# Scores of four heads together in the second cross-attention: 32-row groups, four banks for one group, eight probability buffers

## The reference

```python
EMBED, HEADS, HEAD_DIM = 256, 16, 16
q = proj(query, Wq, bq)      # 8 x 16 heads x 112 x 16
k = proj(key, Wk, bk)        # 8 x 16 heads x 375 x 16
v = proj(value, Wv, bv)
attn = jnp.einsum('bhqd,bhkd->bhqk', q, k) / jnp.sqrt(jnp.float32(Dh))
attn = jax.nn.softmax(attn, axis=-1)
out = jnp.einsum('bhqk,bhkd->bhqd', attn, v)
out = out.transpose(0, 2, 1, 3).reshape(B, -1, D)
out = jnp.einsum('bsd,ed->bse', out, Wo) + bo
```

## Time and profile before

| | us |
|---|---|
| median of 3 runs | 842.96 |
| lowest and highest | 840.47, 846.47 |
| the profiled execution | 840.59 |
| its span, first to last instruction | 838.8 |

### The profile page before, as it was taken

How to read it: one execution, slowest core, us unless ns; L and a number is a source line. 1 busy time by engine, 2 the same in 40 slices (tenths; PEclk the granted TensorE clock), 3 DMA queues, 4 the chain that set the end, 5 groups by cost and what they waited for, 6 DMA issues and landing times.

```text
span 838.8 us, 14453 instructions
## 1 busy us (share of the span) xinstructions
PE 776.1 (93%) x5152; PEld 563.4 (67%) x5152; DVE 460.1 (55%) x1144; ACT 360.5 (43%) x958; POOL 195.6 (23%) x281
## 2 busy tenths in 40 slices
PE   0499999999999999999999997999999987999998
PEld 0345555665555666799898985666666655889976
DVE  2466667667557421122222225847777798598742
ACT  0345565555456512232233323467777767212110
POOL 4312320322100034000000006605444455410000
PEclk9999999999999999899999999899999999999999
DMA  7422142111111593156555423320000000000001
GB/s 217 165 67 55 49 147 78 48 46 46 36 28 34 175 367 117 57 200 203 199 182 188 162 71 105 124 98 2 2 2 2 2 2 1 1 1 1 1 12 34
DMA packets 43419, 69.74 MB, mean 83 GB/s; under 512 B 6499, under 2 KB 34924, under 8 KB 43092
## 3 DMA queue, kind: packets, MB, share of 16 engines
q1 hardware_dynamic: 41812, 65.14, 24.1%
q0 software_dynamic: 1536, 3.67, 1.4%
HBM read 52.56 MB, written 8.26 MB: 73 GB/s over the span
## 4 chain that ended last, share of the span: by engine, by line
PE 77%; DVE 10%; DMA 6%; issue 3%; POOL 2%; ACT 1%; SPq 1%; DVEq 0%; POOLq 0%; ACTq 0%
PE ps L1335 12%; PE ps L1574 7%; PE ps L1771 7%; PE ps L1586 7%; PE ps L1386 6%; PE ps L1389 6%; PE ps L1667 6%; PE ps L1426 4%; PE ps L1505 3%; DMA OT<-slot_rows 3%; PE ps L1808 3%; PE ps L1446 3%; PE ps L1494 3%; PE ps L1692 3%; PE ps L1376 2%
## 5 line engine op out<-in xcount | busy, mean ns | idle before, releaser
L1335 PE MATMUL ps<-ident,arena 112*125 112x112 f32 (+5 forms) x776 | 108.7, 278 | 26.2 <-POOL arena L405 18.7
L1335 PEld LDWEIGHTS ps<-ident,arena 112*125 112x125 f32 (+5 forms) x776 | 86.8, 164 | 54.2 <-issue 35.8
L715 ACT ACTIVATE OT<-ps,bt 128x128 f32<-128x128 f32 x168 | 47.9, 368 | 113.6 <-PE ps L1574 112.7
L744 ACT ACTIVATE arena<-ps,negmax 112x375 f32<-112x375 f32 x128 | 73.1, 571 | 32.3 <-DVE negmax L909 31.8
L1574 PE MATMUL ps<-OT,arena 128*128 128x128 f32 x672 | 80.6, 280 | 0.2 <-DVE OT L1046 0.2
L1574 PEld LDWEIGHTS ps<-OT,arena 128*128 128x128 f32 x672 | 78.8, 196 | 0.6 <-issue 0.6
L1771 PE MATMUL ps<-arena_r 128*112 128x384 f32 x384 | 77.0, 349 | 1.9 <-DVE acc L1143 1.1
L909 DVE TENSOR_REDUCE negmax<-ps 112x1 f32<-112x375 f32 x128 | 63.9, 541 | 23.3 <-PE ps L1667 21.8
L1586 PE MATMUL ps<-arena,OT 128*128 128x256 f32 x336 | 75.8, 379 | 0.0
L904 DVE TENSOR_REDUCE negmax<-ps 112x1 f32<-112x487 f32 x64 | 39.5, 659 | 62.3 <-PE ps L1426 62.3
L1060 DVE COPY yo<-ps 128x256 f32<-128x256 f32 x21 | 8.9, 424 | 108.0 <-PE ps L1586 108.0
(11 more groups left out here) (249 smaller groups left out, 1316.0 us busy)
## 6 DMA issues: line engine op xcount, KB each, us to landing
arena<-in_up_w SPq DMA_DIRECT2D x21, 1024.0 KB, 5.1
arena<-in_down_w SPq DMA_DIRECT2D x8, 1024.0 KB, 10.8
arena<-arena SPq DMA_DIRECT2D x128, 60.9 KB, 2.0
arena<-in_wqkv SPq DMA_DIRECT2D x1, 3072.0 KB, 12.4
arena<-in_ctx SPq DMA_DIRECT2D x8, 375.0 KB
slot_rows<-acc SPq DMA_DIRECT2D x3, 896.0 KB, 7.4
OT<-slot_rows SPq DMA_DIRECT2D x21, 128.0 KB, 4.8
slot_out<-yo SPq DMA_DIRECT2D x21, 128.0 KB, 1.7
```

Of the source, the lines that this page charges most:

```text
L715: act.activation(he[:, i % 2, m, :], ps[:, 2 * (i % 2) + m // 4, (m % 4) * SLOT:(m % 4 + 1) * SLOT], ACT.Gelu, bias=bt[:, i % 3, m:m + 1]) ...
L744: act.activation(probs1[:, h % 4, :], ps[0:TQ, S_BANKS[h % 4], 0:TK], ACT.Exp, bias=negmax[0:TQ, h % 4:h % 4 + 1], accum_out=rsum1[:, n % ...
L1335: return pe.transpose(dst, src, ident[0:k, 0:k])
```

## The change

Scores: the loop goes over v, four groups of four heads in a batch. The four heads of a group lie in four row groups of 32 rows each, with one matmul each, and each has one of the four banks; the group waits until all exponentials of the group before are done. `HEADS` is reordered so that four heads at consecutive places lie in the four row groups.

Probabilities: eight buffers instead of four. Four are the old ones, four are tables and scratch of earlier stages (`cos_t`, `sin_t`, `rt`, `acc`). An exponential waits for the head eight before it.

Transposes: the first two heads of a group go to banks 2 and 3 and are copied by DVE, the last two go to the same banks and are copied by ACT. In a step PE does the scores of group v, then the transposes of the first two heads of the group before, then the values of the group two before, then the transposes of the other two heads, which wait for DVE's copies. DVE does four maxima and then the two copies; ACT does four exponentials and then its two.

The rest is moved: queries of the next batch behind the transposes of step 1 (PE) and in step 2 (DVE), inverse sums in step 0, logits and output scaling in step 1, projection in step 2 (PE), rows and `l1_norm` in step 3, `l1_x` and its copy in step 0 of the batch after. Gating pieces and `w_high` come two in a step. On POOL `f_rows(0)` and `f_rows(1)` come ahead of `w_low(3)` to `w_low(5)`, and the remaining `w_low` behind batch 7. Behind the loop, the first expert products wait for all exponentials, and `l1_ot(7)` on DVE follows `l1_logits(6)`.

```diff
@@ POOL
-                    for i in range(3, 8):
-                        w_low(i)
                     f_rows(0)
                     f_rows(1)
+                    for i in range(3, 6):
+                        w_low(i)
...
@@ ACT
             def l1_exp(n, h):
                 g = n * H1 + h
                 act.wait_ge(L1["max"], g + 1)
-                if positive(g - 3):
-                    act.wait_ge(L1["pt"], g - 3)
+                if g >= 8:
+                    act.wait_ge(L1["pt"], g - 7)
...
-            def l1_step(n, u):
-                l1_exp(n, 2 * u)
-                if n or u:
-                    l1_pt(n * H1 + 2 * u - 2)
-                l1_exp(n, 2 * u + 1)
-                if n == 7 and u == 6:
+            def l1_step(n, v):
+                g = n * H1 + 4 * v
+                l1_exp(n, 4 * v)
+                l1_exp(n, 4 * v + 1)
+                l1_exp(n, 4 * v + 2)
+                if n == 7 and v == 3:
                     gate_exp(0)
-                if n and u == 6:
+                l1_exp(n, 4 * v + 3)
+                if g:
+                    l1_pt(g - 2)
+                    l1_pt(g - 1)
+                if n >= 2 and v == 0:
+                    l1_x(n - 2)
+                if n and v == 3:
                     l1_norm(n - 1)
...
@@ DVE
+            def l1_step(n, v):
+                g = n * H1 + 4 * v
+                l1_max(n, 4 * v)
+                l1_max(n, 4 * v + 1)
+                l1_max(n, 4 * v + 2)
+                l1_max(n, 4 * v + 3)
+                if g:
+                    l1_pt(g - 4)
+                    l1_pt(g - 3)
+                if n + 1 < B and v == 2:
+                    l1_q(n + 1, (n + 1) % 2)
+                if n and v == 0:
                     l1_sums(n - 1)
-                if n >= 2 and u == 2:
+                if n >= 2 and v == 1:
                     l1_logits(n - 2)
-                if n and u == 3:
+                if n and v == 1:
                     l1_ot(n - 1)
-                if nxt and u == 4:
-                    l1_q(n + 1, 1 - p)
-                if n and u == 5:
+                if n and v == 3:
                     l1_rows(n - 1)
...
@@ PE
+            def l1_s(n, v):
+                g = n * H1 + 4 * v
+                if v == 0:
                     pe.wait_ge(L1["qe"], (n + 1) * KC)
-                if g >= 4:
-                    pe.wait_ge(L1["exp"], g - 2)
-                for r in (0, 1):
-                    h = HEADS[2 * u + r]
-                    pe.matmul(ps[0:TQ, S_BANKS[(2 * u + r) % 4], 0:TK], qm[p][64 * r:64 * r + 64, h, :],
-                              kT[64 * r:64 * r + 64, n, h // 8, :], start=True, stop=True,
-                              tile_position=(64 * r, 0)).then_inc(L1["s"], 1)
+                if g:
+                    pe.wait_ge(L1["exp"], g)
+                for i in range(4):
+                    h, rows = HEADS[4 * v + i], slice(32 * i, 32 * i + 32)
+                    pe.matmul(ps[0:TQ, S_BANKS[i], 0:TK], qm[n % 2][rows, h, :], kT[rows, n, h // 8, :],
+                              start=True, stop=True, tile_position=(32 * i, 0)).then_inc(L1["s"], 1)
 
             def l1_pt(g, h):
                 pe.wait_ge(L1["exp"], g + 1)
-                if g >= 2:
-                    pe.wait_ge((s_pta, s_ptv)[g % 2], g // 2)
+                if g % 4 >= 2:
+                    pe.wait_ge(s_ptv, g // 4 * 2 + g % 2 + 1)
+                elif g >= 4:
+                    pe.wait_ge(s_pta, g // 4 * 2 - 1 + g % 2)
...
+            def l1_step(n, v):
+                g = n * H1 + 4 * v
+                l1_s(n, v)
+                if g:
+                    l1_pt(g - 4, (g - 4) % H1)
+                    l1_pt(g - 3, (g - 3) % H1)
+                if n >= 2 and v == 0:
+                    l1_x(n - 2)
+                if n >= 2 and v == 1:
+                    l1_g(n - 2)
+                if v >= 2:
+                    l1_pv(n, v - 2)
+                elif n:
+                    l1_pv(n - 1, v + 2)
+                if n and v == 1:
                     l1_rT(n - 1)
...
+                if g:
                     l1_pt(g - 2, (g - 2) % H1)
-                if nxt and u == 3:
+                    l1_pt(g - 1, (g - 1) % H1)
+                if n + 1 < B and v == 1:
                     l1_q(n + 1)
-                if n and u == 5:
+                if n and v == 2:
                     l1_o(n - 1)
...
@@
-HEADS = [8 * c + 2 * i + o for c in range(2) for o in range(2) for i in (0, 2, 1, 3)]
+HEADS = [8 * c + 2 * i + o for c in range(2) for o in range(2) for i in range(4)]
```

More of the change, by code:

```diff
@@ L169, in build @@
         vm, qm = (vm_0, vm_1), (qm_0, qm_1)
+        pb = [probs1[:, h, :] for h in range(4)] + [
+            cos_t[0:TQ, 0:TK], sin_t[0:TQ, 0:TK], rt[:, :, :].rearrange("p k n -> p (k n)")[:, 0:TK],
+            acc[:, :, :].rearrange("p t d -> p (t d)")[:, 12 * P:12 * P + TK]]
         NEAR = 5
@@ L550, in _ @@
                         w_low(i)
-            for i in range(8, 16):
+            for i in range(6, 16):
                 w_low(i)
@@ L1126, in l1_pt @@
                     dve.wait_ge(L1["pv"], g // 4 - 1)
-                dve.tensor_copy(pT1[:, g % 8, :], ps[0:CR, 3, 0:3 * TQ]).then_inc(s_ptv, 1)
+                dve.tensor_copy(pT1[:, g % 8, :], ps[0:CR, 2 + g % 2, 0:3 * TQ]).then_inc(s_ptv, 1)
             def l1_rows(n):
@@ L1309, in _ @@
             l1_logits(6)
+            l1_ot(7)
             f_mix(0, 0, 0)
```

72 lines of the change are left out of this document (25 added, 47 removed).

## The result

The changed kernel takes **856.0 us** (median of four runs, 851.2 to 856.8) where the kernel before takes 842.1: ratio 1.0145, 95% interval 1.0091 to 1.0199. It is slower by 14 us; the forecast was 841.5, no difference, with a range of 830 to 856, at whose edge the median lies. The profiled execution has 856.78 us, 855.0 of span, mean granted clock 0.970; before it had 840.59, 838.8 and 0.988.

A forecast was written before the change was run, and what follows sets the result against it. It took TensorE to bound batches 1 to 5 before, and the chain through VectorE's copies after the change. 2.2 + 0 + 1.2 - 1.0 - 3.8 = -1.4 took 842.96 to 841.5 us, range 830 to 856.

The forecast's parts named there:

- half rate: Rival: four score banks written at once halve each stream, every step 0.82 us longer, 867 us; chance 0.12.
- two and two: Rival: a group's first two heads come as now, the others 0.82 us later, 848 us; chance 0.10.
- four increments: Semaphore increments of a score group, four where two stood: estimated 149 against 87 ns, 2 us more over 32 steps.
- plain step: Step of four heads without extra work: 4.15 us, set by VectorE's copies, with 3.2 us of TensorE work.
- step 0: First step of a batch: exponentials wait for ScalarE's normalisation of the rows, 5.2 us.
- batch 0: First batch of the stage, without rows to normalise: 17.25 us against 15.03, +2.2.
- Batches 1 to 5: Steady part of the stage: no change in the first of them, +0.3 us in each other, +1.2.
- steps 1 and 2: Second and third step, with next queries and output projection behind the last transposes: 5.05 and 5.0 us.
- Batch 6: Batch that gets gating pieces on VectorE, two in a step, charged 0.3 us: 19.7 against 20.68, -1.0.
- End of the stage: Last batch up to its last values, with the hand-over: 27.65 us against 31.48, -3.8, a 3.42 us wait gone.
- the clock: Rival: TensorE idles about 18% of each batch and its clock falls, 2 us each time, +12, 853 us; chance 0.12.
- TensorE stays the bound: Rival: VectorE and ScalarE find their slack, every batch 3.3 us shorter, 817 us or anything between; chance 0.12.

The follow-up runs named there:

- run 3: Changed kernel with VectorE's copy of the first head's transposed probabilities moved ahead of the third maximum; 854.4 us, ratio 1.016.
- run 1: Changed kernel plus small products that nothing reads, placed in TensorE's idle time; 855.5 us, ratio 1.017.
- run 4: Changed kernel with the edits of run 3 and run 1 together, the moved copy and unread products; 847.6 us, ratio 1.008.
- run 7: Changed kernel with the edits of run 1 and run 5 together, unread products and gate pieces respread; 846.2 us, ratio 1.0075.
- run 9: Kernel before, with a pair's scores waiting for both exponentials of the pair just before; 927.2 us, ratio 1.105.
- run 2: Changed kernel with scores back in 64 rows, one pair behind the other, and the old order of heads; 854.2 us, ratio 1.0155.
- run 5: Changed kernel with the gate's fifteen VectorE pieces placed by a table, away from GpSimd's queries product of batch 6; 853.6 us, ratio 1.018.
- run 11: The kernel of run 10 without its unread products; 849.8 us, ratio 1.013.
- run 10: The kernel of run 8 with the gate's fifteen pieces spread once more; 841.0 us, ratio 1.0021.
- run 6: Kernel before, with each pair's scores read from two 32-row groups instead of two of 64 rows; median 893.9 us against 839.8.
- run 12: The kernel of run 10 with next queries and output projection moved behind the following scores, and fewer unread products; 833.1 us, ratio 0.989.
- run 8: The kernel of run 7 with ScalarE's normalization behind step 0's exponentials and the transposes of x at that step's end; 841.5 us, ratio 1.0023.

## Why the prediction was wrong, point by point

**Right, with its number.** The score group costs 0.83 us (0.82 predicted; bounds 0.82 to 1.64), so 32-row groups run side by side as pairs do. The Trainium skill, TensorE: Matmul & The Clock Gate, section "Measured speedup vs the span model", has 3.07 times for four 32-row tiles, from which the prediction's estimate was 1.07. This case's trace has 0.83, and the measurement decides on the cost; what one head alone takes no run shows, so the factor itself is not measured. The first maximum starts 0.91 us after the scores (621.07 to 621.98), 0.92 predicted: the rivals of half rate and of two and two are out, and no cost of four increments shows in these numbers. VectorE's copies set the step (run 3), the third head's transposes start at 3.39 (3.3), ScalarE waits 1.6 us for GpSimd ahead of the normalization and step 0 takes 5.01 (5.2), TensorE idles 0.94 us in a plain step (0.9), batch 0 without a fall takes 17.62 (17.25). Without a fall batch 7 and the hand-over take 27.42 us (27.65), the 3.42 us wait there being gone.

**Wrong by size: the terms of the sum.** These I take from stretches without a fall, in after or in runs 1, 4 and 7, whose steps are the same.

- Batch 0: +2.6 us (17.62 against 15.03), +2.2 predicted.
- Batches 1 to 5: 19.05 + 19.94 + 19.72 + 20.28 + 19.73 = 98.7 against 95.3 (571.32 to 666.60), +3.4; +1.2 predicted. The plain step is 4.28 and not 4.15, since the third head's transposes start at 3.39 and not 3.3 and the next scores 0.9 us behind them; steps 1 and 2 are 5.18 and 5.26 and not 5.05 and 5.0; and batch 4 is 0.55 us longer than its neighbours, with GpSimd's 2.9 us operation for the gate's constants (L506) in it, which I had not looked at; that this operation is the cause is not shown.
- Batch 6: 21.49 against 20.68, +0.8; -1.0 predicted. The failed step is "two pieces fit there, except in step 3": pieces stood beside GpSimd's product of the queries and took 1.56 and 1.64 us. The row to have used was at hand, 2.60 us for such an operation beside GpSimd; I used it only where the stall goes.
- End of the stage: 27.42 against 31.48, -4.1; -3.8 predicted.

Sum: +2.8 and not -1.4. So 4 us of the miss are structure, and the change would have been level within 1% on them alone.

**Wrong in kind: the clock.** After's falls cost 2.05 us in batch 0 (19.67 against 17.62), 4.0 in batch 4 (24.27 against 20.28) and 6.3 at the end (33.73 against 27.42), 12.3 us together. 2.8 + 12.3 = 15.1, and 14.9 is what the stage lost. The forecast had this as a rival, with +12 us, 853 and a chance of 0.12. The mechanism was right. That its +12 is met so closely is luck: it stood for six or seven falls of 2 us each, and there were four, of 2.05 and 4.0 us and two of 6.3 together. What failed is the sentence that held the rival down, "Against: idle stretches now are 0.9 to 1.3 us", in two ways.

- It leaves out the longer stretches: 2.98 us in batch 0's first step, which its own sum has as 3.9 us with 0.82 us of scores in it, 1.53 at the hand-over, and 2.58 in batch 6, which the wrong term above hides. Three of the four falls, 8.3 of the 12.3 us, come behind or in these.
- Short stretches can do it too. Batch 4's fall, 4.0 us, has none over 1.06 us near it, and run 9, with none over 1.48 us but 30% of the batch idle, has seven falls. In after's steady steps, idle 16%, it is rare: in the profiles of after and of runs 2, 3, 5 and 11, five kernels of this kind without unread products, batches 1 to 5 are 25 batches and have this one fall.

Runs 4, 7 and 10 do nothing but fill idle time, long and short, against runs 3, 5 and 11, and each is 7 to 9 us faster for it; how this divides between long and short stretches was not tried. The Trainium skill, TensorE: Matmul & The Clock Gate, section "A second HAM failure mode: psum-queue depth-cycling", describes a kernel whose matmul groups leave small idle times while it cycles through PSUM banks and whose clock goes up and down for that; it speaks for this rival, and I had not weighed it. Run 9's trace agrees with it, with stretches of up to 1.48 us and 72 us at half clock.

Was it the idle time alone? Theory A said so and run 6 contradicted it: with TensorE busy and half of the rows unused during scores, the clock was down for 130 us of the profiled execution. The kernel after uses all rows in a group of four, so it has only the idle part of the trouble; run 2, with 64 rows, more busy time and a higher mean clock in all four runs, agrees with both. What is shown: idle time alone does it (run 9), unused rows alone do it (run 6, its second fall), added work takes 7 to 9 us away in three pairs of kernels (3 and 4, 5 and 7, 11 and 10), though not between after and run 1, where the stall of batch 6 stayed. What stays open: when a fall starts and how long it lasts. It differs between executions of one kernel (827.8 to 839.5 us for run 12), and between kernels with the same steps. The sizes of single falls are each from one profiled execution.

**The rival that TensorE stays the bound** (817, 0.12) didn't come, since what is saved on TensorE becomes idle time as long as four maxima and two copies stand between a group and its last transposes. But its main thought, that the freed time can be used, holds: run 12 stands at a ratio of 0.989 where run 10 stood at 1.002, by TensorE's order and fewer unread products, and its executions at a clock of 0.990 (827.8 to 830.4) are 8 to 12 us below the kernel before at 0.990 to 0.992 (838.2 to 839.9).

## What to carry to other kernels

Time taken from the bounding engine is only a gain if something else fills it: look for work that stands behind the chain and can stand in it (run 12, 1.9 us a batch), and move it before judging the change. If TensorE goes from full to partly idle, price its clock as a case of its own: here it turned 3 us of loss into 14. List all idle stretches from the forecast's own steps, the first step and the hand-over among them and not only the steady ones; test the clock by filling idle time with unread products, and count the rows that each matmul uses. Keep small VectorE operations away from a long GpSimd product where a chain waits for VectorE, and look where a moved operation lands: run 5 took a stall of 2.58 us out and made one of 3.52.

## What the runs showed of the hardware that was not expected

- Two 32-row tiles in place of two 64-row tiles, with the same instructions, time at full clock and busy share: from 839.8 us to 862.6 in one run and 893.8 to 894.8 in three. In one of the latter TensorE ran at 1.2 GHz for 85.3 us in a row while busy for 86.98 of 88.30 us. Once down, it stayed down although TensorE worked without a pause, and having come back to 2.4 GHz it fell again at 691.5, still without a pause.
- VectorE operations of 64 columns take 0.19 to 0.24 us alone. Beside a GpSimd product some take 0.37 to 1.64 (2.60 in the kernel before), while a reduction of 64 columns kept its 0.22. The copy of 256 columns takes 0.29 alone and 3.37 to 3.41 beside one, at the hand-over of after, of run 4 (L1231 in both) and of run 8 (L1232).
